# Source one-hots of an edge count: from one vector comparison to two activations on another engine

## The reference

```python
x = x + _L0_gnn_ref(_layernorm(x), ..., node_type_24, src, dst)   # encoder, two GAT layers
x = x + _L0_ffn_ref(_layernorm(x)[None], ...)[0]                  # 8 experts, top 1, capacity
x = x + _L1_gnn_ref(_layernorm(x), src, dst, ...)                 # gated sums over edges
x = x + _L1_ffn_ref(_layernorm(x)[None], ...)[0]                  # 8 heads, top 1
```

```python
feat = (h @ W.T).reshape(-1, H, HID)
e = leaky_relu(el[src] + er[dst], 0.2)
a = exp(e - m[dst]) / segment_sum(exp(e - m[dst]), dst)
out = segment_sum(a[:, :, None] * feat[src], dst) + bias
```

## Time and profile before

| | us |
|---|---|
| runs: median of 3 | 4710.1 |
| runs: lowest, highest | 4685.79, 4713.58 |
| the profiled execution | 4669.19 |
| its span, first to last instruction | 4667.5 |
| loops of the edge counting within it, from 481.1 to 918.7 | 437.6 |

### The profile page before, as it was taken

The page is one execution under the profiler, slowest core; times in us unless marked ns, Lnnn a source line. Parts: engine busy times, 40 slices in busy tenths (PEclk is TensorE's granted clock), DMA queues, the critical chain, the costliest instruction groups (busy, mean ns, idle before and its releaser), DMA issues. The chain is left out here.

```text
span 4667.5 us, 61585 instructions
## 1 busy us (share of the span) xinstructions
PE 3664.4 (79%) x20551; PEld 1983.5 (42%) x20552; DVE 2758.5 (59%) x5295; ACT 905.6 (19%) x1933; POOL 1101.4 (24%) x1166
## 2 busy tenths in 40 slices
PE   0898566599996999736978668888888888868695
PEld 0455111133344434323643234444444444458585
DVE  3333999999985999840026455555555555577001
ACT  0232000000000000001210023333333333335231
POOL 0000000000000000001014366666666666600202
PEclk9999777799995999857975589999999999989798
DMA  1300000000001000003221155555555555750102
GB/s 62 95 11 17 1 1 1 1 28 19 10 10 48 10 19 12 3 9 118 87 67 50 44 160 163 168 166 162 164 161 166 166 163 161 157 131 10 54 31 71
DMA packets 215165, 347.33 MB, mean 74 GB/s; under 512 B 102139, under 2 KB 142569, under 8 KB 213313
## 3 DMA queue, kind: packets, MB, share of 16 engines
q0 software_dynamic: 79968, 260.10, 20.1%
q1 hardware_dynamic: 120518, 73.23, 5.3%
q10 hardware_dynamic: 14492, 11.60, 0.8%
HBM read 301.44 MB, written 43.93 MB: 74 GB/s over the span
## 5 line engine op out<-in xcount | busy, mean ns | idle before, releaser
L1755 POOL DMA_INDIRECT gated_G<-tab_d,ixall x880 | 889.9, 1011 | 532.4 <-DVE gated_sv L1785 261.2
L953 PE MATMUL dense_p_o<-dense_W,feat 128*32 128x512 f32 (+1 forms) x8400 | 880.7, 543 | 28.3 <-DVE dense_W L895 28.1
L895 DVE SCALAR_TENSOR_TENSOR dense_W<-dense_B,steep,cnt 128x512 f32<-128x512 f32 (+1 forms) x1400 | 849.0, 680 | 61.5 <-PE dense_p_o L953 48.9
L1837 PE MATMUL gated_p_sg<-gated_sv,gated_oh 128*128 128x512 f32 x1760 | 823.7, 612 | 0.4 <-DVE gated_sv L1785 0.4
L953 PEld LDWEIGHTS dense_p_o<-dense_W,feat 128*32 128x32 f32 x8400 | 361.9, 109 | 518.0 <-DVE dense_W L895 231.4
L1781 DVE TENSOR_TENSOR gated_tv<-gated_G,gated_p_b 128x1024 f32<-128x1024 f32 x220 | 268.7, 1221 | 441.2 <-DMA ffn_out_d<-experts_ye 262.3
L1837 PEld LDWEIGHTS gated_p_sg<-gated_sv,gated_oh 128*128 128x128 f32 x1760 | 333.9, 201 | 340.5 <-issue 334.8
L1828 PE MATMUL gated_p_b<-wr,gated_ohT 128*128 x2640 | 372.2, 296 | 49.0 <-issue 43.5
L760 PE MATMUL count_p_c<-count_R,count_L 128*128 128x500 bf16 x784 | 275.8, 490 | 161.7 <-DVE count_L L722 161.7
L1806 ACT ACTIVATE gated_sv<-gated_tv 128x1024 f32<-128x1024 f32 x220 | 232.5, 1057 | 635.8 <-DVE gated_tv L1781 522.7
L1325 POOL MEMSET route_up<- 128x128 f32 x1 | 0.2, 206 | 1495.4 <-POOLq L130 1495.4
(11 more groups left out here) (359 smaller groups left out, 4035.7 us busy)
## 6 DMA issues: line engine op xcount, KB each, us to landing
experts_ew<-in_ew SPq DMA_DIRECT2D x16, 1024.0 KB
gated_G<-tab_d,ixall POOLq DMA_INDIRECT x880
dense_B<-rise_d SPq DMA_DIRECT2D x12, 1024.0 KB
dense_Wd<-in_fWd ACTq DMA_DIRECT2D x1, 8192.0 KB
tab_d<-feat SPq DMA_DIRECT2D x50, 128.0 KB, 2.5
tab_d<-gated_in_rowg SPq DMA_DIRECT2D x25, 256.0 KB
ffn_in_d<-encode_zero POOLq DMA_DIRECT2D x1, 4096.0 KB, 16.7
xs_d<-encode_zero POOLq DMA_DIRECT2D x1, 4096.0 KB, 27.1
```

The source lines that it names most:

```text
L895: o = nc.vector.scalar_tensor_tensor(out=out, in0=rise, scalar=C.steep[:, q * H + h:q * H + h + 1], in1=count, op0=ALU.max, op1=ALU.mult)
L953: m = nc.tensor.matmul(p_o[c % 2][h * MT:(h + 1) * MT, a, 0:n], feat[:, q, h, lo:lo + MT], W[t % 2][:, h, 0:n], start=(q == 0), stop=(q == ...
L1755: gp.indirect_dma_start(out=G[g % UN][:, j, :], out_offset=None, in_=C.tab3[:, :], in_offset=bass.IndirectOffsetOnAxis(ap=C.ix[:, g * ET + ...
L1837: t = nc.tensor.matmul(p_sg[k % 2][:, :], oh[k][:, j, :], sv[k % 2][:, j, :], start=(j == 0), stop=(j == ET - 1))
```

## The change

The comparison that makes `L` leaves DVE's stream. ACT gets a stream in this stage: for each group four activations write `away`, the distance |iota - low| of each tile in bf16 (`lowT` now holds the negative, so that it is a bias), and after a wait for these four a fifth writes `L` = relu(1 - away) for all four tiles, which is 1 at distance 0 and 0 elsewhere. Before it writes, it waits for PE's products of two groups ago. PE waits for `R` and `L` by two semaphores. DVE makes one memset more, for the constant 1 that the fifth activation has as its bias. `away` exists twice. Nothing changes in the other stages.

```diff
+            def _(act):
+                act.wait_ge(s_one, 1)
+                act.wait_ge(s_tab, 2)
+                for g in range(CG):
+                    k = g % 2
+                    i, p = divmod(g, CP)
+                    if g >= 2:
+                        act.wait_ge(s_L, g - 1)
+                    for j in range(ET):
+                        nc.scalar.activation(away[k][:, j, :], C.iota[:, :], ACT.Abs, bias=lowT[:, i, j * CP + p:j * CP + p + 1]).then_inc(s_away, 1)
+                    act.wait_ge(s_away, (g + 1) * ET)
+                    if g >= 2:
+                        act.wait_ge(s_cnt, g - 1)
+                    nc.scalar.activation(L[k][:, :, :], away[k][:, :, :], ACT.Relu, bias=one[:, 0:1], scale=-1.0).then_inc(s_L, 1)
...
+                nc.vector.memset(one[:, :], 1.0).then_inc(s_one, 1)
...
-                nc.vector.scalar_tensor_tensor(out=low[:, :, :], in0=hi[:, :, :], scalar=float(-P), in1=pr[:, :, :, 0], op0=ALU.mult, op1=ALU.add).then_inc(s_low, 1)
+                nc.vector.scalar_tensor_tensor(out=low[:, :, :], in0=hi[:, :, :], scalar=float(P), in1=pr[:, :, :, 0], op0=ALU.mult, op1=ALU.subtract).then_inc(s_low, 1)
...
-                    nc.vector.tensor_tensor(L[k][:, :, :], C.iota[:, :].unsqueeze(1).broadcast_to([P, ET, P]),
-                                            lowT[:, i, :].rearrange("p (j q) -> p j q", q=CP)[:, :, p:p + 1].broadcast_to([P, ET, P]), ALU.is_equal).then_inc(s_oh, 1)
...
-                    pe.wait_ge(s_oh, (g + 1) * (ET + 1))
+                    pe.wait_ge(s_oh, (g + 1) * ET)
+                    pe.wait_ge(s_L, g + 1)
```

More of the change, by code:

```diff
@@ L655, in stage_count @@
         ramp = sb("ramp", [P, CK], I32); ramp16 = sb("ramp16", [P, CK], U16)
-        L = [sb(f"L{k}", [P, ET, P], BF16) for k in range(2)]; R = [sb(f"R{k}", [P, ET, CK], BF16) for k in range(2)]
+        L = [sb(f"L{k}", [P, ET, P], BF16) for k in range(2)]; away = [sb(f"away{k}", [P, ET, P], BF16) for k in range(2)]; one = sb("one", [P, 1]); R = [sb(f"R{k}", [P, ET, CK], BF16) for k in range(2)]
         p_k = ps("p_k", [P, 2, 512]); p_l = ps("p_l", [P, 2, 512]); p_m = ps("p_m", [P, 512]); p_d = ps("p_d", [1, 512])
@@ L661, in stage_count @@
         s_tab = sem("s_tab"); s_oh = sem("s_oh"); s_cnt = sem("s_cnt"); s_add = sem("s_add")
+        s_one = sem("s_one"); s_away = sem("s_away"); s_L = sem("s_L")
         words = NB * CN // 4
@@ L738, in _ @@
                     add(g)
+            @block.scalar
+            def _(act):
[12 more added lines that the diff above has]
+                    nc.scalar.activation(L[k][:, :, :], away[k][:, :, :], ACT.Relu, bias=one[:, 0:1], scale=-1.0).then_inc(s_L, 1)
             @block.tensor
```

## The result

On the chip of the first timing the changed kernel took 4644.72 us (median of 4 runs, 4625.87 to 4648.94) against 4702.91 for the kernel before (4 runs): ratio 0.9872, 95% interval 0.9829 to 0.9915. Timed once more on another chip it took 4417.6 against 4476.46 us, ratio 0.9868 with interval 0.9853 to 0.9884. So it is 58 and 59 us faster. The forecast was 60 us less, 4650 us; its base of 4710.1 was the median of three runs, and 4702.91 is the median with a fourth.

The account below looks back on a forecast made before the run. The prediction took DVE as the bound before and ACT after: 196 x (2.224 - 1.92) = 60 us with 0.5 at the start, about 60, so 4710.1 - 60 = 4650 us, range 4600 to 4680.

Parts of the forecast that it names:

- The bound before: Edge-counting loops: DVE sets the pace without holes, 2.22 us a group, of which the comparison for L takes 0.60.
- ACT's group: ACT's five activations per group in the counting loops: 1.93 us, rounded to 1.92, bounds 1.79 to 2.12, above DVE's 1.62.
- distance of two Abs: Between starts of neighbouring Abs on ACT: 0.29 us, bounds 0.26 and 0.32.
- hop to Relu: ACT's wait for its own four Abs before Relu: 0.05 us, bounds 0.03 to 0.10.
- PE and the queue: Products and queued register reads in the loops: no added time at 1.92 us; low-clock slow stretches show from 1.79.
- The sum: Whole program: 60 us saved, from 196 groups going from 2.224 to 1.92 us, and 0.5 at the start.
- DVE's idle time: In the counting loops after the change: rises to 55 to 65 us, put down to PE's products.
- PE's idle time: In the counting loops after the change: put down to waiting for L on ACT; no size given.
- ACT at 1.98 or more: Rival: ACT's group in the loops takes 1.98 to 2.22 us, saving under 47 us; chance 0.20.
- DVE's 1.62: Rival: the loops' group falls to DVE's 1.62 us or just above, saving 118 us, time 4592; chance 0.05.
- load of a table: Rival: table loads between Abs and Relu at 1.28 us each add some 430 us; chance 0.01.
- The slower one: Rival: ACT's activations reading SBUF don't overlap, group 2.37 us, time 4739; chance 0.05.

Follow-up runs that it names:

- stagger: Changed kernel with the first Abs of group g+1 issued between the last Abs and the Relu of group g; 4388.19 us, ratio 0.9810 to the kernel before.
- pipe: Changed kernel with ACT computing all four Abs of group g+1 before the Relu of group g, still two buffers; 4413.12 us.
- act_more: Changed kernel with a fifth, unread Abs of 128 columns per group on ACT; 4470.94 us, ratio 0.9993 to the kernel before.
- alt: stagger, with DVE also making the fourth tile of L in every second group; 4374.72 us, ratio 0.9780 to the kernel before.
- split: Changed kernel with DVE making the fourth tile of L in every group and ACT the other three; 4388.16 us.
- dve_less: Changed kernel with DVE making three of four R per group, the fourth product reusing the first R (wrong counts); 4416.21 us.

## Why the prediction was right

**The bound before** held: DVE without a hole, 0.60 us a group for L. With the comparison gone DVE would run at 1.62. The changed kernel shows that pace by itself near the start, for six groups (additions from 491.92 to 501.66), while ACT still had a lead from the start, where DVE and PE had waited for products at the low clock:

```profile
493.55 0.67 DVE L731 TENSOR_TENSOR cnt<-cnt,count_p_c 128x500 f32 x1
...
495.17 0.67 DVE L731 TENSOR_TENSOR cnt<-cnt,count_p_c 128x500 f32 x1
...
496.80 0.67 DVE L731 TENSOR_TENSOR cnt<-cnt,count_p_c 128x500 f32 x1
```

**ACT's group** was put at 1.93 and rounded to 1.92 us; it is 1.92. The terms, forecast and measured: Abs 0.40 and 0.386; distance of two Abs 0.29 and (1.26 - 0.386) / 3 = 0.291; hop to Relu 0.05 and 0.04; Relu 0.72 and 0.721; what it holds of ACT 0.61 and 0.62. Abs and the hop were each put 0.01 too high and Relu's share 0.01 too low, and the rounding from 1.93 down to 1.92 had no row behind it; that the sum agrees to the last digit is luck, worth 2 us. The choice of 0.29 over the 0.26 of activations that read PSUM was the one that mattered, 3 x 0.03 us x 196 = 18 us.

The estimate by the Trainium skill (ScalarE: Activation LUTs, What ACT_TABLE_LOAD costs) had 387 ns for an Abs and 93 ns of overlap between neighbours; the trace agrees, with 386 ns and 386 - 291 = 95.

**PE and the queue** don't come in between, as forecast, though PE's clock was at the low level for part of the time (mean 0.87). Before 504.36 DVE's addition waited 0.99 us for products at the low clock, and Relu went on 1.92 to 1.93 us apart:

```profile
501.60 0.72 ACT L754 ACTIVATE count_L<-count_away,count_one 128x512 bf16<-128x512 bf16 x1
...
503.52 0.72 ACT L754 ACTIVATE count_L<-count_away,count_one 128x512 bf16<-128x512 bf16 x1
...
504.36 0.68 DVE L731 TENSOR_TENSOR cnt<-cnt,count_p_c 128x500 f32 x1 [0.99 <-PE count_p_c L777]
...
505.45 0.72 ACT L754 ACTIVATE count_L<-count_away,count_one 128x512 bf16<-128x512 bf16 x1
```

The prediction also said that PE's slow stretches would begin to show at a group of 1.79 us. That stays untested: at 1.78 us, in `stagger`, the mean clock was 0.99, so there were hardly any such stretches left.

**The sum** was 60 us; the loops lost 61.4 and took 376.8, in the forecast 375 to 380; the medians lost 58 and 59. Placing it on the median and not on the profiled execution was right: the gated layer of that execution was 37 us shorter than in the profile after, which has nothing to do with this stage.

**What was off.** DVE's idle time was forecast at 55 to 65 us and its busy time at 317; they were 46 and 331. The 317 is 196 x 1.62, a sum of distances of starts, which holds only where each instruction overlaps the next. Where the addition waits for products it no longer overlaps the R ahead of it: in the lines from 602.20 on, R ends at 603.32 and the addition starts at 603.53. So the busy time of such a group is up to 0.09 us more, and the idle time less by as much. PE's idle time was to be put down to L on ACT; of 138.3 us only 21.9 were, see below. And the first estimate of what ACT's wait for itself costs (0.05) counted only the hop; the overlap that it forbids is 0.09 more. This did not change the sum, which had both lengths in it, but `pipe` was drawn up as if the wait ahead of Relu were the only one.

**The rivals.** ACT at 1.98 or more (0.20) and DVE's 1.62 (0.05) did not come, and no load of a table stands in the loops (0.01). The slower one (0.05) did not come either: neighbours on ACT overlap by 95 ns in this form too. ACT needs 1.92 us for what DVE did in 0.60, and the move still gains, since ACT was idle. How near it was, `act_more` shows: 0.29 us more on ACT and hardly anything is gained. The Trainium skill (ScalarE: Activation LUTs, Rules for kernel authors) says to use VectorE for relu; this case agrees that DVE is the faster engine for this work, but not that the move is a loss.

## What to carry to other kernels

Work that is moved to an idle engine is paid in full on that engine: sum its stream from distances of starts. Where two buffers let the engines run apart, as here, the new pace is the larger of the two engines' sums. An activation that waits for the one directly ahead of it cost 0.13 to 0.14 us more here than one that doesn't, whether it reads what that one wrote (Relu behind Abs) or writes what that one read (Abs behind Relu in `pipe`). One independent instruction in between removed the cost; moving the wait to another neighbour didn't. Once two engines are nearly level, try giving single tiles from one to the other, as `alt` did.

## What the runs showed of the hardware

- PE's mean granted clock in the loops was higher the closer together the groups came: 0.77 with groups 2.22 us apart, 0.79 at 2.21 (`act_more`), 0.87 at 1.92, 0.99 at 1.78 and at 1.70. A group's products took 1.02 us at the high clock in all of them; what nearly went are the long ones, 1.85 us at 1.2 GHz. In `split`, `stagger` and `alt` PE's products took 199 to 201 us in all, in the kernel before 276.
- A wait of PE for two semaphores was put down by the profile mostly to R on DVE or to "issue". `dve_less` shows that it was not R, and the start of PE's products 0.10 us behind the end of each Relu shows that it was L on ACT.
- An Abs of 128 columns that reads SBUF took 386 ns, with starts 291 ns apart; the activations of the same width that read PSUM took 369 ns, with starts (1.14 - 0.369) / 3 = 0.257 us apart. Their outputs differ in type (bf16 and f32), so the source is not the only difference.
- The gated layer, which gathers rows by DMA, took 1429 and 1466 us on one chip and 1232 to 1238 on the two others, with the same instructions.
